# A decoder kernel: the last batch of attention shared out anew, its outputs scaled in parts, the maximum over partitions moved

## The chip, the cores and the metric

The kernel is one program on 1 core of a Trainium2 chip, with its five engines (TensorE, VectorE, ScalarE, GpSimd, and SyncE, which issues the DMAs). The metric is the device time of one execution in microseconds (us): 1484.29 us before, the median of 3 runs (1482.04 to 1485.83). In the profile's rows PE is TensorE, DVE VectorE, ACT ScalarE, POOL GpSimd and SP SyncE.

## The reference

A decoder block on x of 16 batches x 256 rows x 512 columns, with three sublayers, each on the layer norm of x and each added to x:

```python
x = x + attn(_layernorm(x), w_qkv, w_proj)             # 16 heads of 32, causal, weights and activations rounded
x = x + xattn(_layernorm(x), k, fside_S2_0, ctx, ctx, 8)  # a long convolution per head, done as matrix products
x = x + ffn(_layernorm(x), gate_w, up_w, down_w, ...)  # silu(gate) * up, then down, weights in fp8
```

What matters here is how attention ends. The output `out` of a row is divided by the softmax's sum, then `_bitlinear(out, w_proj)` rounds it with a scale of its own per row: `s = 127 / max|out|`, `round(out * s) / s`. So the maximum over all 16 heads of a row must be known before the first element is rounded. The second sublayer starts with the layer norm of the sum, and every product in it needs rows of all 16 batches, the last one too.

## The kernel before

Part 1 is attention. It runs over pairs of heads: batch b has 8 pairs, pair n = 8b + p, 128 in all, the last batch being pairs 120 to 127 (PAIRS = 8, B = 16). Every engine has its own program, written out as a loop over steps t, and a stage of pair n is issued at step t = n + its lag (EXP 9, HIGH 10, LOW 11, WEIGH 12, WEIGHED 13). The order on an engine is that of its loop, and only semaphores tie the engines together. For a pair: TensorE writes transposed scores into a PSUM tile of two banks (`probabilities`, L628 to 652), ScalarE takes the exponential into `pT` (L1433), one engine casts it to fp16, the high part `pH` (ScalarE at L1439 for 7 pairs of 8, VectorE at L1011 for the first), GpSimd subtracts to get the low part `pL` (L1796), TensorE multiplies both with the values (`weigh`, 12 products of 65 columns, L668 and L669), ScalarE copies the result out of PSUM into `oraw` (L1447). `s_kq` is one buffer, so the scores of pair n wait for the exponential of n - 1; `pT` and `pH` are three buffers, `pL` two.

When a batch has its 8 pairs, `finish` on VectorE and ScalarE takes it on: `oraw` has two halves to be added (tile 0 on VectorE, tile 1 on GpSimd, L1801), the product with the reciprocal sums gives `o_sb`, then the maximum, step, reciprocal step, rounding on ScalarE, a transpose on TensorE, a copy on ScalarE, the projection (L684) and on VectorE the addition to x (`add_out`, L1045). The last batch has `finish_last` (VectorE L1048 to 1077, ScalarE L1477 to 1496), which does this for tile 0 (rows 0 to 127) first and then for tile 1, with an `add_out` of the batch before between. ScalarE there computes steps and rounds both tiles before it copies the first transpose.

Then the rows of the last two batches go by DMA into `x_grp`, and part 2 begins: layer norm statistics of head 0 on VectorE (L1182 to 1187), `rstd` and shift on GpSimd (L1845, L1847), scaling on ScalarE (L1608), transpose, and the outer products `kv`: blocks 0 and 1 of head 0 on VectorE (L1194), blocks 2 and 3 on GpSimd (L1866). TensorE multiplies them with the taps (`mix`, L803): of each head first row block 0 (needs kv block 0), then row block 2 (blocks 0, 1, 2 in this order), then 1, then 3, each in two halves.

Beside this, GpSimd takes once the maximum over partitions of 4 numbers (L1837), whose result bounds a scale used much later (`fuse_bound`, seven small VectorE instructions, L1288 to 1301). It comes on GpSimd after the last low part and the last addition, ahead of the layer norm of part 2. Two banks of 128x512 fp32 and a third (`misc`) go round among transposes and projections; who takes one waits for the release of the use three before.

## Time and profile before

| | us |
|---|---|
| median of 3 runs | 1484.29 |
| the profiled execution | 1481.37 |
| its span | 1479.6 |
| TensorE busy | 1391.8 (94%) |
| VectorE busy | 1233.3 (83%) |
| GpSimd busy | 1178.9 (80%) |
| ScalarE busy | 871.6 (59%) |

The span is 1.77 us shorter than its own execution's time. Attention fills the first 462 us or so, the seam to part 2 lies at 462 to 482, and everything later is part 2. Busy shares over the whole span say little about the seam; it is read from the chain of waits and from each engine's rows in order of time, where brackets give the idle time before an instruction and what ended it.

### The profile page before, as it was taken

How to read it: one execution, taken by the hardware profiler on the slowest of the kernel's cores; microseconds unless marked ns; L12 is line 12 of the kernel's file. 1: busy time of each engine (PE TensorE's matmuls, PEld its weight loads, DVE VectorE, ACT ScalarE, POOL GpSimd, SP SyncE). 2: the span in 40 equal slices, each digit the busy share in tenths (PEclk: the TensorE clock that was granted, in tenths of full speed). 3: DMA queues.
4: the chain of work that ended last, by engine and by line, in shares of the span. 5: the costliest groups of instructions: out<-in, count | busy, mean ns of one | idle time of the engine just before them, and what ended most of it. 6: DMA issues, size and time to landing. Idle time of an engine off the chain costs nothing.

```text
span 1479.6 us, 23950 instructions
## 1 busy us (share of the span) xinstructions
PE 1391.8 (94%) x8405; PEld 773.0 (52%) x8405; DVE 1233.3 (83%) x1964; ACT 871.6 (59%) x1437; POOL 1178.9 (80%) x902
## 2 busy tenths in 40 slices
PE   3788999999986997999999999999999999999998
PEld 2677878787863442334444444444444444444443
DVE  6889999999884898899898899899889889888511
ACT  5689999999885123544455545464455446544341
POOL 3389999999985787888888888878887888888532
PEclk9899999999997999999999999999999999999999
DMA  5654646464622533222513421432323232240001
GB/s 193 155 126 117 171 133 172 136 171 122 158 67 75 173 79 88 55 57 64 107 44 72 89 61 43 93 78 50 79 65 77 62 76 57 65 100 15 21 15 29
DMA packets 171587, 133.57 MB, mean 90 GB/s; under 512 B 120500, under 2 KB 124748, under 8 KB 171468
## 3 DMA queue, kind: packets, MB, share of 16 engines
q1 hardware_dynamic: 171276, 131.91, 35.6%
q8 instruction: 67, 1.10, 0.3%
q14 instruction: 52, 0.43, 0.1%
q10 hardware_dynamic: 192, 0.14, 0.1%
HBM read 50.67 MB, written 19.92 MB: 48 GB/s over the span
## 4 chain that ended last, share of the span: by engine, by line
PE 65%; DVE 11%; POOL 8%; issue 7%; ACT 6%; DMA 1%; SPq 0%; POOLq 0%; DVEq 0%; ACTq 0%
PE gu L844 20%; PE gu L858 11%; PE shared_bank L789 9%; POOL pL L1796 3%; PE y L811 3%; PE y L808 3%; PE y L805 3%; PE y L813 3%; PE y L814 3%; DVE blockmax L987 2%; DVE o_sb L1027 2%; PE gu L803 1%; PE y L803 1%; DVE qkt L967 1%; ACT pH L1439 1%
## 5 line engine op out<-in xcount | busy, mean ns | idle before, releaser
L1668 ACT ACTIVATE shared<-shared_bank 128x512 f32<-128x512 f32 x162 | 96.2, 594 | 322.9 <-PE shared_bank L789 322.9
L1219 DVE TENSOR_TENSOR y<-shared,y 128x512 f32<-128x512 f32 x324 | 224.1, 692 | 42.7 <-ACT shared L1668 23.0
L1796 POOL TENSOR_TENSOR pL<-pT,pH 128x768 f16<-128x768 f32 x128 | 216.8, 1696 | 13.6 <-ACT pH L1439 7.7
L1226 DVE TENSOR_REDUCE oT<-z 128x64 f32<-128x512 f32 x256 | 175.6, 686 | 8.7
L844 PE MATMUL gu<-fT,wg 128*128 128x512 f16 x768 | 181.4, 379 | 1.5 <-DMA fT<-fnl 1.5
L844 PE MATMUL gu<-fT,wu 128*128 128x512 f16 x768 | 182.5, 381 | 0.0
L1222 DVE TENSOR_TENSOR z<-y,cT 128x512 f32<-128x512 f32 x236 | 162.4, 688 | 11.0 <-PE y L803 4.4
L1930 POOL TENSOR_TENSOR fuL<-fu,fuH 128x512 f16<-128x512 f32 x96 | 112.0, 1166 | 71.7 <-ACT fuH L1683 71.5
L858 PE MATMUL gu<-wd,fuH 128*128 128x512 f16 x384 | 145.5, 379 | 0.0
L858 PE MATMUL gu<-wd,fuL 128*128 128x512 f16 x384 | 145.5, 379 | 0.0
L1866 POOL TENSOR_TENSOR kv<-vT,cT 128x1024 f32<-128x1024 f32 x70 | 137.8, 1970 | 6.1 <-ACT vT L1623 6.1
L844 PEld LDWEIGHTS gu<-fT,wg 128*128 128x128 f16 x768 | 75.0, 98 | 120.5 <-issue 47.4
L844 PEld LDWEIGHTS gu<-fT,wu 128*128 128x128 f16 x768 | 75.5, 98 | 119.5 <-issue 47.2
L1433 ACT ACTIVATE pT<-s_kq,ws 128x768 f32<-128x768 f32 x128 | 115.0, 898 | 26.9 <-PE s_kq L651 20.2
L987 DVE TENSOR_REDUCE blockmax<-s_qk 128x6 f32<-128x768 f32 x124 | 117.6, 948 | 3.9 <-PE s_qk L621 2.7
L789 PE MATMUL shared_bank<-kv_sum,toep 128*128 128x512 f32 x216 | 111.2, 597 | 0.3 <-POOL kv_sum L1854 0.3
L1854 POOL TENSOR_TENSOR kv_sum<-kv 128x1024 f32<-128x1024 f32 x27 | 63.7, 2360 | 55.2 <-DVE kv L1194 55.2
L637 PE MATMUL s_kq<-pack 128*128 128x128 f16 x768 | 99.4, 220 | 0.0
L1241 DVE SCALAR_TENSOR_TENSOR fu<-gu,cols,sil 128x512 f32<-128x512 f32 x96 | 71.4, 743 | 33.6 <-PE gu L844 33.6
L1789 POOL TENSOR_TENSOR qkhl<-qkt,qkhl 128x512 f16<-128x512 f32 x62 | 83.9, 1354 | 19.2 <-ACT qkhl L1419 19.2
L1439 ACT ACTIVATE pH<-pT 128x768 f16<-128x768 f32 x112 | 94.0, 840 | 0.0
L1194 DVE TENSOR_TENSOR kv<-vT,cT 128x1024 f32<-128x1024 f32 x58 | 75.1, 1297 | 14.2 <-ACT vT L1631 11.5
(231 smaller groups left out, 3561.8 us busy)
## 6 DMA issues: line engine op xcount, KB each, us to landing
pack<-qkhl SPq DMA_DIRECT2D x256, 128.0 KB, 2.6
x_sb<-in_x SPq DMA_DIRECT2D x16, 512.0 KB, 4.0
c_sb<-in_ctx SPq DMA_DIRECT2D x32, 256.0 KB, 4.0
hankel<-in_L_xattn_k SPq DMA_DIRECT2D x32, 256.0 KB, 4.1
out_y<-yo SPq DMA_DIRECT2D x32, 256.0 KB, 2.9
x_grp<-x_scratch SPq DMA_DIRECT2D x30, 256.0 KB, 3.5
x_scratch<-x_sb SPq DMA_DIRECT2D x14, 512.0 KB, 3.0
wraw<-in_L_attn_w_qkv SPq DMA_DIRECT2D x3, 1024.0 KB, 9.6
```

Source lines behind the costliest of these rows:

```text
L789: T.matmul(shared_bank[:], tap(h, (2, 0, 1)[part]), (kv_sum, kv12, kv_sum)[part][:, half * HB:(half + 1) * HB, :, :].rearrange("p b j i -> ...
L844: made = T.matmul(bank[:], (wg, wu)[which][:, cb, ib * P:(ib + 1) * P], fT[:, cb, part, :], start=cb == 0 and part == 0, stop=cb == CB - 1 ...
L858: made = T.matmul(bank[:], src[:, t * P:(t + 1) * P], wd[:, ib, :], start=ib == 0 and part == 0, stop=ib == IB - 1 and part == 1)
L987: V.tensor_reduce(out=blockmax[b % 2][:, p, :], in_=score_tile(n)[:, 0:6, :], op=ALU.max, axis=AXIS.X, negate=True).then_inc(max_done, 1)
L1219: chain.step(V.tensor_tensor(bank[:], shared[2 * part + half][:], bank[:], op))
L1222: V.tensor_tensor(z[:], y, weight, ALU.mult).then_inc(m_zm, 1)
L1226: V.tensor_reduce(out=oT[h % 2][:, lb, own].rearrange("p (b j) -> p b j", b=HB), in_=z[:], op=ALU.add, axis=AXIS.X).then_inc(m_z, 1)
L1433: S.activation(pT[n % NP][:], s_kq[:, 0:6, :], ACT.Exp, scale=ws[:, 4:5]).then_inc(exp_done, 1)
L1439: S.activation(pH[n % NP][:], pT[n % NP][:], ACT.Copy).then_inc(high_act, 1)
L1796: G.tensor_tensor(pL[n % 2][:], pT[n % NP][:], pH[n % NP][:], ALU.subtract).then_inc(low_done, 1)
L1866: G.tensor_tensor(block(h, lb), vT[:, lb, :].rearrange("p (b i) -> p b i", b=B).unsqueeze(2).broadcast_to([P, B, M_POS, M_POS]), cT[h % 2] ...
L1930: G.tensor_tensor(fuL[ib][:], fu[n % 2][:], fuH[:, ib, :], ALU.subtract).then_inc(f_fl, 1)
```

## The change

Pairs 119, 121, 123, 125 and 127 get their low part on VectorE instead of GpSimd, and pair 127 its high part on VectorE instead of ScalarE. From pair 121 on the scores of odd pairs go to `s_qk`, which the row maxima no longer need, so that a pair's scores wait for the exponential two before. VectorE's `finish_last` starts three steps earlier (LAST_AT, after the low part of pair 127) and works on tile 0 in three parts: heads 0 to 7, heads 8 to 13, heads 14 and 15, each with its reciprocal, addition (for the first part on GpSimd, `sum_first`), product and maximum, then a maximum over the three; steps are computed on VectorE too, and outputs lie in `xn`. Its `add_out` of the batch before comes after tile 1. On ScalarE the first transpose is copied ahead of the rounding of tile 1, and the copies of taps and context for head 0 (`turn_taps`, `copy_cT`), once ahead of the last high part, come here; so does `turn_c` on TensorE. GpSimd's maximum over partitions comes behind the layer norm of head 0, and `fuse_bound` at step 8 of part 2.

```diff
-    HIGH_ON_ACT = (1, 2, 3, 4, 5, 6, 7)
+    HIGH_ON_ACT, LAST_HIGH_ON_ACT = (1, 2, 3, 4, 5, 6, 7), (1, 2, 3, 4, 5, 6)
...
+        LAST_AT = B * PAIRS - 1 + LOW
+        LAST_PARTS = ((0, PAIRS // 2), (PAIRS // 2, PAIRS - 1), (PAIRS - 1, PAIRS))
+        LOW_ON_DVE = [n for n in range((B - 1) * PAIRS - 1, B * PAIRS) if n % 2 == 1]
...
+        def scores_tile(n):
+            return s_qk if n > (B - 1) * PAIRS and n % 2 == 1 else s_kq
...
+        FUSE_BOUND_AT, SCALE_DOWN_AT = 8, 20
...
-                w.wait_ge(exp_done, n)
-                T.matmul(s_kq[:, 0:4, :], ident_b[:], mask_kq[:], start=True, stop=False)
+                if n > (B - 1) * PAIRS:
+                    w.wait_ge(exp_done, n - 1)
+                    w.wait_ge(max_done, B * PAIRS)
+                else:
+                    w.wait_ge(exp_done, n)
+                to = scores_tile(n)
...
                     elif k == 0:
+                        turn_c(0, misc1)
                         turn_oq(b, 0)
...
+            def low_part(n):
+                w.wait_ge(*high_done(n))
+                w.wait_ge(pv_pe, n - 1)
+                V.tensor_tensor(pL[n % 2][:], pT[n % NP][:], pH[n % NP][:], ALU.subtract).then_inc(low_last, 1)
...
+                for i, (begin, stop) in enumerate(LAST_PARTS):
+                    first, end = 2 * begin, 2 * stop
+                    w.wait_ge(pv_out, PAIRS * b + stop)
+                    chain.step(V.reciprocal(rl[:, 0, first:end], raw[:, 0, first:end, D]))
+                    if i == 0:
+                        w.wait_ge(o_sum, B)
+                    else:
+                        chain.step(V.tensor_tensor(raw[:, 0, first:end, 0:D], raw[:, 0, first:end, 0:D], raw[:, 0, first:end, VW:VW + D], ALU.add))
+                    chain.wait()
+                    if stop < PAIRS:
+                        chain.step(scale_heads(0, first, end))
+                        chain.wait()
+                        chain.step(V.tensor_reduce(out=inv[:, i:i + 1], in_=xn[:, 0, first * D:end * D], op=ALU.max, axis=AXIS.X,
+                                                   apply_absolute_value=True))
...
+                        chain.step(V.tensor_scalar(am[:, 0:1], am[:, 0:1], inv[:, 0:1], inv[:, 1:2], ALU.max, ALU.max))
+                step_last(0)
...
+                step_last(1)
+                w.wait_ge(c2_done, b)
+                add_out(b - 1, 0)
                 w.wait_ge(c2_done, b + 1)
                 add_out(b, 0)
                 add_out(b - 1, 1)
...
-                if k == 1:
-                    fuse_bound()
...
+                if g == FUSE_BOUND_AT:
+                    fuse_bound()
...
                 for t in range(NT):
-                    w.wait_ge(omax_done, b + t + 1)
-                    S.activation(step[:, t:t + 1], am[:, t:t + 1], ACT.Copy, scale=1.0 / 127.0).then_inc(ostep_done, 1)
                     w.wait_ge(oscale_done, b + t + 1)
...
                     if t == 0:
...
+                        projected(w)
+                        turn_taps(0)
+                    copy_oqT(b, t)
+                    if t == 0:
+                        copy_cT(0, misc1)
...
+            def sum_first():
+                raw, heads = oraw[(B - 1) % 2], slice(0, 2 * LAST_PARTS[0][1])
+                w.wait_ge(pv_out, PAIRS * (B - 1) + LAST_PARTS[0][1])
+                G.tensor_tensor(raw[:, 0, heads, 0:D], raw[:, 0, heads, 0:D], raw[:, 0, heads, VW:VW + D], ALU.add).then_inc(o_sum, 1)
...
-                if t == REDUCE_AT:
-                    w.wait_ge(mx_done, 1)
-                    G.partition_all_reduce(mall[:], mx[:], P, RMAX).then_inc(mall_done, 1)
...
                     G.tensor_tensor(shift, shift, rstd, ALU.mult).then_inc(m_shift, 1)
+                    if h == 0:
+                        w.wait_ge(mx_done, 1)
+                        G.partition_all_reduce(mall[:], mx[:], P, RMAX).then_inc(mall_done, 1)
```


On GpSimd, from the last low parts (pL) to the first kv block of part 2. The rows named ISA are the switches of GpSimd's program and, with mall, the maximum over partitions. Before:

```order
L1796 TENSOR_TENSOR pL<-pT,pH 128x768 x5
L1801 TENSOR_TENSOR oraw<-oraw 128x16x32
L1837 ISA
L1837 ISA mall<-mx 128x4
L1845 ISA
L1845 TENSOR_TENSOR mstat<-mstat,minus_half 128x1
L1847 TENSOR_TENSOR mstat<-mstat 128x1
L1866 TENSOR_TENSOR kv<-vT,cT 128x1024
```

And after the change, same place:

```order
L1839 TENSOR_TENSOR pL<-pT,pH 128x768 x2
L1844 TENSOR_TENSOR oraw<-oraw 128x8x32
L1849 TENSOR_TENSOR oraw<-oraw 128x16x32
L1892 TENSOR_TENSOR mstat<-mstat,minus_half 128x1
L1894 TENSOR_TENSOR mstat<-mstat 128x1
L1897 ISA
L1897 ISA mall<-mx 128x4
L1916 ISA
L1916 TENSOR_TENSOR kv<-vT,cT 128x1024
```

Three low parts are gone from the run of five, and both switches with the maximum now stand between the layer norm (mstat) and the kv block, block 2 of head 0.

On VectorE, from the low part of pair 125 to the rounding step of tile 0, after the change:

```order
L1033 TENSOR_TENSOR pL<-pT,pH 128x768
L1067 SCALAR_TENSOR_TENSOR x_sb<-misc,osmall,x_sb 128x512
L1058 RECIPROCAL osmall<-osmall 128x2
L1028 CAST pH<-pT 128x768
L1067 SCALAR_TENSOR_TENSOR x_sb<-misc,osmall,x_sb 128x512
L1033 TENSOR_TENSOR pL<-pT,pH 128x768
L1078 TENSOR_SCALAR xn<-ones,ws 128x2
L1093 RECIPROCAL osmall<-oraw 128x8
L1081 TENSOR_TENSOR xn<-oraw,osmall 128x256
L1102 TENSOR_REDUCE osmall<-xn 128x1
L1093 RECIPROCAL osmall<-oraw 128x6
L1097 TENSOR_TENSOR oraw<-oraw 128x6x32
```

Before, the two additions to x stood there alone, and after them the undivided work. Now the last low part is queued behind them and ahead of all parts of tile 0, of which the third follows.

On ScalarE, from the last copy of `oraw`, before:

```order
L1447 ACTIVATE oraw<-pv 128x2x130
L1475 ACTIVATE oqT<-misc 128x4x128
L1486 ACTIVATE osmall<-osmall 128x1
L1488 ACTIVATE o_sb<-o_sb,osmall 128x512
L1494 ACTIVATE osmall<-osmall,ws 128x1
L1486 ACTIVATE osmall<-osmall 128x1
L1488 ACTIVATE o_sb<-o_sb,osmall 128x512
L1475 ACTIVATE oqT<-misc 128x4x128
```

And after:

```order
L1495 ACTIVATE oraw<-pv 128x2x130
L1523 ACTIVATE oqT<-misc 128x4x128
L1534 ACTIVATE xn<-xn,osmall 128x512
L1536 ACTIVATE osmall<-osmall,ws 128x1
L1552 ACTIVATE toep<-hankel 128x512
L1523 ACTIVATE oqT<-misc 128x4x128
L1559 ACTIVATE cT<-misc 128x512
L1534 ACTIVATE xn<-xn,osmall 128x512
```

The copy of tile 0's transpose no longer stands behind the step and the rounding of tile 1, but behind the taps' copy.

## Rows read from the trace of the kernel before

**Rows 1.** Busy time by stretch: us from the start, engines, clock, DMA.

```profile
462.00:472.00 10.00, 5.36 (x18) 2.44 (x17) 5.65 (x10) 3.53 (x9) 1.45 (x2) 0.67 0.17 47
482.00:492.00 10.00, 10.00 (x23) 4.37 (x23) 8.17 (x14) 1.41 (x2) 5.38 (x5) 0.74 0.88 282
```

**Rows 2.** Chain of waits, 425 to 500: start us, us, what.

```profile
450.42 4.24 POOL pL L1796 x2
...
475.76 0.71 issue
```

**Rows 3.** GpSimd in order of time: start, us, engine, line, operation, [idle before <-releaser].

```profile
442.21 1.81 POOL L1805 TENSOR_TENSOR fw_raw<-fw_raw,fw_pow 128x768 f32<-128x768 f32 x1
443.98 2.09 POOL L1796 TENSOR_TENSOR pL<-pT,pH 128x768 f16<-128x768 f32 x1
...
450.42 5.83 POOL L1796 TENSOR_TENSOR pL<-pT,pH 128x768 f16<-128x768 f32 x3
...
458.68 1.64 POOL L1796 TENSOR_TENSOR pL<-pT,pH 128x768 f16<-128x768 f32 x1 [0.58 <-ACT pH L1439]
...
469.17 0.39 POOL L1837 PARTITION_ALL_REDUCE mall<-mx  x1 [5.79 <-issue]
476.47 0.59 POOL L1845 TENSOR_TENSOR mstat<-mstat,minus_half 128x1 f32<-128x1 f32 x1 [6.92 <-DVE mstat L1187]
477.14 0.19 POOL L1847 TENSOR_TENSOR mstat<-mstat 128x1 f32<-128x1 f32 x1
480.25 2.99 POOL L1866 TENSOR_TENSOR kv<-vT,cT 128x1024 f32<-128x1024 f32 x1 [2.92 <-ACT vT L1623]
...
486.34 1.95 POOL L1866 TENSOR_TENSOR kv<-vT,cT 128x1024 f32<-128x1024 f32 x1
```

**Rows 4.** GpSimd's switches of its program, one line's query.

```profile
L1837 POOLq MODIFY_POOL_CONFIG  x2: 11/11/11, 463.3 to 463.4; - x2
L1845 POOLq MODIFY_POOL_CONFIG  x2: 82/82/83, 469.5 to 469.5; - x2
```

**Rows 5.** VectorE in order of time, 420 to 500.

```profile
443.77 0.80 DVE L1021 TENSOR_TENSOR oraw<-oraw 128x512 f32<-128x512 f32 x1
450.55 2.60 DVE L1027 TENSOR_TENSOR o_sb<-oraw,osmall 128x1024 f32<-128x1024 f32 x1 [5.98 <-POOL oraw L1801]
...
463.96 0.69 DVE L1063 TENSOR_TENSOR o_sb<-oraw,osmall 128x512 f32<-128x512 f32 x1
...
465.73 0.17 DVE L1070 RECIPROCAL osmall<-osmall 128x1 f32<-128x1 f32 x1 [0.35 <-ACT osmall L1486]
...
475.25 0.18 DVE L1184 BATCH_NORM_AGGREGATE mstat<-mstat 128x2 f32<-128x6 f32 x1
475.47 0.15 DVE L1186 TENSOR_SCALAR mstat<-mstat 128x1 f32<-128x1 f32 x1
...
480.21 4.11 DVE L1194 TENSOR_TENSOR kv<-vT,cT 128x1024 f32<-128x1024 f32 x2 [2.31 <-ACT vT L1623]
```

**Rows 6.** ScalarE in order of time, 420 to 500.

```profile
449.53 0.90 ACT L1433 ACTIVATE pT<-s_kq,ws 128x768 f32<-128x768 f32 x1 [0.97 <-POOL pL L1796]
...
461.85 0.39 ACT L1447 ACTIVATE oraw<-pv 128x260 f32<-128x260 f32 x1
...
465.92 0.72 ACT L1488 ACTIVATE o_sb<-o_sb,osmall 128x512 f32<-128x512 f32 x1 [0.23 <-DVE osmall L1070]
...
468.97 0.58 ACT L1475 ACTIVATE oqT<-misc 128x512 bf16<-128x512 f32 x1
```

**Rows 7.** TensorE in order of time, two stretches.

```profile
469.69 3.57 PE L684 MATMUL misc<-wprojT,oqT 128*128 128x512 bf16 x8 [1.88 <-ACT oqT L1475]
...
481.58 3.75 PE L803 MATMUL y<-kv,toep 128*128 128x512 f32 x4 [2.11 <-DVE kv L1194]
485.12 3.77 PE L803 MATMUL gu<-kv,toep 128*128 128x512 f32 x6
```

**Rows 8.** VectorE in order of time, 500 to 530.

```profile
502.69 0.69 DVE L1222 TENSOR_TENSOR z<-y,cT 128x512 f32<-128x512 f32 x1 [2.02 <-PE y L803]
```

More of the change, by code:

```diff
@@ L675, in turn_oq @@
                 for cb in range(CB):
-                    made = T.transpose(bank[:, cb * P:(cb + 1) * P], o_sb[:, t, cb * P:(cb + 1) * P], ident[:])
+                    made = T.transpose(bank[:, cb * P:(cb + 1) * P], (o_sb if b < B - 1 else xn)[:, t, cb * P:(cb + 1) * P], ident[:])
                 made.then_inc(oqT_pe, 1)
@@ L1073, in finish_last, with scale_heads @@
-                w.wait_ge(ostep_done, b + 2)
-                V.reciprocal(inv[:, 1:2], step[:, 1:2]).then_inc(oscale_done, 1)
+                w.wait_ge(xqT_pe, 2 * B)
+                w.wait_ge(c2_done, b - 1)
+                chain.step(V.tensor_scalar(xn[:, :, C], ones[:, 0:NT], ws[:, 1:2], EPS, ALU.mult, ALU.mult))
+                def scale_heads(t, first, end):
+                    return V.tensor_tensor(xn[:, t, first * D:end * D].rearrange("p (h d) -> p h d", d=D), raw[:, t, first:end, 0:D],
+                                           rl[:, t, first:end].unsqueeze(2).broadcast_to([P, end - first, D]), ALU.mult)
@@ new lines, in step_last @@
+                def step_last(t):
+                    chain.wait()
+                    V.tensor_scalar(step[:, t:t + 1], am[:, t:t + 1], 1.0 / 127.0, None, ALU.mult).then_inc(ostep_done, 1)
+                    w.wait_ge(ostep_done, b + t + 1)
+                    V.reciprocal(inv[:, t:t + 1], step[:, t:t + 1]).then_inc(oscale_done, 1)
+                for i, (begin, stop) in enumerate(LAST_PARTS):
[9 more added lines that the diff above has]
+                        chain.step(scale_heads(0, first, end))
+                        chain.wait()
+                        chain.step(V.tensor_reduce(out=inv[:, i:i + 1], in_=xn[:, 0, first * D:end * D], op=ALU.max, axis=AXIS.X,
+                                                   apply_absolute_value=True))
+                    else:
+                        scale_heads(0, first, end).then_inc(o_mult, 1)
+                        w.wait_ge(o_mult, b + 1)
+                        chain.step(V.tensor_reduce(out=am[:, 0:1], in_=xn[:, 0, first * D:C + 1], op=ALU.max, axis=AXIS.X,
+                                                   apply_absolute_value=True))
+                        chain.wait()
+                        chain.step(V.tensor_scalar(am[:, 0:1], am[:, 0:1], inv[:, 0:1], inv[:, 1:2], ALU.max, ALU.max))
@@ L1141, in vector_program @@
                         low_max(use)
-                if (n := pair(t, HIGH)) is not None and n % PAIRS not in HIGH_ON_ACT:
+                if (n := pair(t, LOW)) in LOW_ON_DVE:
+                    low_part(n)
+                if (n := pair(t, HIGH)) is not None and not high_on_act(n):
                     high_part(n)
@@ L1552, in scalar_program @@
                     copy_weights(i, blocks)
-                if (n := pair(t, HIGH)) is not None and n % PAIRS in HIGH_ON_ACT:
+                if (n := pair(t, HIGH)) is not None and high_on_act(n):
                     high_part(n)
@@ L1820, in gpsimd_program @@
             for t in STEPS:
-                if (n := pair(t, LOW)) is not None:
+                if (n := pair(t, LOW)) is not None and n not in LOW_ON_DVE:
                     low_part(n)
+                if t == LAST_AT:
+                    sum_first()
                 for b, k in batches(t, FINISH, 1):
```

82 lines of the change are left out of this document (31 added, 51 removed).

## The prediction

> **What bounds the kernel now.** I read the chain of waits first, as it says which engine ends each stretch, then each engine's rows in order of time for the seam between attention and part 2, then the granted clock by stretch. In the last pairs the chain runs over GpSimd's low parts [rows 2]: three stand back to back from 450.42 to 456.25 [rows 3], and ScalarE sat idle 0.97 us before an exponential until a low part freed its buffer [rows 6]. The last copy of `oraw` ends at 461.85 + 0.39 = 462.24, the rounding of tile 0 starts at 465.92, its transpose is copied at 468.97 [rows 6], the projections start at 469.69 and TensorE's first product of part 2 at 481.58 [rows 7]. From there TensorE works without a gap (10.00 of 10.00 us busy) [rows 1]. So what lies between 450 and 481 is latency, and a microsecond taken out of it is one off the time, unless something new is late at 481.
>
> **Low parts on VectorE.** GpSimd takes 1.64 us for one [rows 3]. VectorE's row for this form is missing. Its product of 512 columns took 0.69, the addition of 512 took 0.80 [rows 5]; 768 columns are 1.5 times that, 1.03 to 1.20, and I take 1.0, since a fixed part doesn't grow. But the engines don't run freely beside each other. VectorE's addition at 443.77 took 0.80, and the low part that GpSimd began at 443.98 took 2.09 instead of 1.64; the product of 1024 columns at 450.55, beside three low parts, took 2.60, where twice 0.69 is 1.38, and the three took 5.83, where 3 x 1.64 is 4.92 [rows 3, 5]. So I add both engines' operations as one queue. From 442.2 on, until the last low part: two operations on a weight piece, 1.81 each (the one in the rows [rows 3] and its like), three low parts left on GpSimd (122, 124, 126) 4.92, an addition there for which I take 1.1, between VectorE's 0.80 for as many columns and GpSimd's 1.64 for 768, four low parts on VectorE 4.0, its addition 0.80 and product 1.38. That is 15.8, so the last low part ends at 458.0. Products and copy follow in 1.9 us (458.68 + 1.64 = 460.32 to 462.24 before) [rows 3, 6]: 459.9, a gain of 2.3. Ends of the range: if operations also wait for their inputs, 1.1 are left; without any blocking, ScalarE and the chain of pair 127 set the end: the exponential at 449.53 could start 0.97 sooner and the two waits of this size that follow go, 3.4.
>
> By the Trainium skill, SBUF — State Buffer, section "SBUF: two separate sides", VectorE with two SBUF inputs and GpSimd hold one pair of ports in turn, each for a whole instruction. The 2.60 and 2.09 agree with it. By that rule the gain is the 2.3; if the two ran freely, it would be the 3.4.
>
> **The second score buffer and the work off ScalarE.** With `s_kq` alone the scores wait for the exponential before, and ScalarE for them; taps, context copy and one high part stood on ScalarE ahead of pair 127. All this shortens ScalarE's way, which the queue above now outlasts. Its gain is inside the 2.3, and outside it nothing.
>
> **Outputs in parts.** From the end of the last `oraw` copy to the rounding 3.68 us go by (465.92 - 462.24) [rows 6]. After: behind its last low part VectorE has four operations each for parts one and two, some 1.3 us for each part (512 columns take 0.69, the parts have 256 and 192, and tiny operations start 0.22 apart, 475.25 to 475.47 [rows 5]), while TensorE and ScalarE need 1.9 us for pair 127. Then seven tiny dependent operations, 7 x 0.22 = 1.54. Low part to rounding 2.6 + 1.54 = 4.1, less 1.9, is 2.2 against 3.68: gain 1.5; where GpSimd's addition of tile 1 gets in between (1.1), 0.4. VectorE must also finish two additions to x ahead of pair 127's parts: I take 0.7, range 0.2 to 1.5.
>
> **ScalarE's order.** From rounding to projection 469.69 - 465.92 = 3.77 us [rows 6, 7], in which the copy of the transpose stood behind tile 1's step and rounding. Without them: rounding 0.72, transposes 0.9 (512 columns take 3.57 / 8 = 0.45, fp32 has two passes [rows 7]), copy 0.58, hand-overs 0.4 = 2.6. But the projection's bank is now the one that `add_out` of batch 14 frees, and that stands behind tile 1 on VectorE: 0.2 + 0.69 + 0.69 + 0.4 + 0.7 + 0.2 = 2.9. Gain 0.8, range 0.5 to 1.1. `turn_c` stands ahead of the transpose on TensorE and runs while the rounding is awaited; taps and context copy fit beside transposes and projection, and if the latter were late, it would be 0.6. SyncE's issues of the last rows keep their order and wait for the same additions; nothing is queued differently there.
>
> **The maximum over partitions.** Before, GpSimd was through at 463.4, the first switch is at 463.3, and the maximum starts at 469.17 after 5.79 us of idle time that has no releaser; the second switch is at 469.5, and the next GpSimd instruction starts at 476.47 [rows 3, 4]. That one waited for VectorE, ready by 475.76: the chain has 0.71 us of "issue" there which nothing else explains [rows 2]. I read it as the end of a second load like the first, from 469.56 to at most 476.47: 5.79 and 6.9 us. Its cover was the wait for the last batch. Moving the maximum behind the layer norm gives back 0.6 (0 to 0.7). But now both loads are queued ahead of kv block 2 of head 0. Call M the end of the shift (477.14 + 0.19 = 477.33 [rows 3]). Block 2 began at M + 2.92 and took 2.99 beside VectorE; alone it takes 1.95 [rows 3]. Now 5.79 + 0.39 + 6.9 = M + 13.1, done at M + 15.05. TensorE's row block 0 starts at 481.58 = M + 4.25. A product has two passes here: four for the two halves of block 0, and six for a half of row block 2, from 485.12 = M + 7.8, of which the fifth needs kv block 2 [rows 7]. It stands there at M + 10.3 (two thirds of 3.77) and waits until M + 15.2: a stall of 4.9 us where there was none. VectorE's own kv blocks end sooner without GpSimd beside them, which helps nobody. All of TensorE's following work moves by it. GpSimd's backlog (block 3, 1.95, and the skip's product) is worked off before head 1's blocks can start, as these wait for a transpose behind the stalled products.
>
> The clock adds to it. The first products ran at the lower of the two levels, 1.2 of 2.4 GHz: granted 0.67 in 462 to 472, 0.74 in 482 to 492 [rows 1], after TensorE had been half idle. Four passes took 3.75, 0.94 each, and at the upper level it would be 0.47 [rows 7]. A stall of 4.9 us invites a second such stretch. Cost of the move: 4.9, plus 0 to 3, and I take 5.8; the least is 0, if the second load is short, and the most 7.8.
>
> The Trainium skill, GPSIMD Engine Reference, section "Instruction dispatch", has a load of about 6 us (5.95) which the first call after a switch pays. The 5.79 agrees; the 476.47 doesn't, if the load began only with that call, as it would be near 481.7. By two loads of 5.95 the stall would be 4.1 instead of 4.9.
>
> `fuse_bound` moves to step 8: seven tiny operations, 7 x 0.22 = 1.5 us, into a place where VectorE idled 2.02 us [rows 8]. Nothing; without that cover 1.5.
>
> **Sum.** Gains 2.3 + 0.7 + 0.8 + 0.6 = 4.4 (1.8 to 6.7); cost 5.8. Net +1.4: the profiled execution's 1481.37 would be 1482.8, and on the median of the runs, 2.9 higher, 1484.29 + 1.4 = 1485.7.
>
> **Rivals.** (A) The second load is short or absent. Then block 2 begins at M + 6.3 and is done at M + 8.3, ahead of its use at M + 10.3: no stall, -4.4, 1479.9 (1477.6 to 1482.5). For it: only 0.71 us of an edge speak of that load. Against it: the first is as plain as can be, and a switch stands ahead of both. (B) Slower: the clock after the stall. TensorE stands until M + 15.2 and then runs at the lower level as long as it did from 481.58, some 6 us for 3 us of work: cost 7.8. It decides wherever the gains stay under 3.3, and with 2.3 the time is +5.5, 1489.8. For it: 0.67 and 0.74 after lesser gaps; against it: it needs weak gains too. (C) The change doesn't do what it says: odd low parts only change the engine in one queue, VectorE's additions to x get late by as much, and attention's pairs and parts together end 1.0 sooner, not 3.0. With the stall 5.8 - 1.0 - 0.8 - 0.6 = +3.4, 1487.7; without it -2.4, 1481.9.
>
> **How the numbers follow.** What this kernel's measurement can tell from no change is 0.3%, 4.5 us, so 1479.8 to 1488.7. The forecast (stall, net -2 to +4.5) has 0.47, of it 0.45 same and 0.02 slower. A 0.27: being on the edge, 0.16 faster, 0.11 same. B 0.12, slower. C 0.14: 0.10 same, 0.02 on either side. That is faster 0.18, same 0.66, slower 0.16; I move 0.04 from same to faster, since the gains reach to 6.7. The range 1478.5 to 1490 leaves out a tenth at each end; the forecast's own is 1482.3 to 1488.7.
>
> **What would show it.** In the changed kernel, from the same start: the last `oraw` copy ends near 459.9 and tile 0's rounding starts near 462.9; a gap on TensorE inside the first six passes of row block 2, of 4 to 5 us, ended by GpSimd's kv; that kv starts 13 us behind the shift. The forecast is wrong if it starts within 7 us of the shift (A), if passes behind the stall still take over 0.8 us (B), or if pair 127's copy ends after 461 (C).

## The result, and the profile after

The changed kernel takes 1489.20 us in the median of 6 runs (1487.30 to 1491.39), the kernel before 1485.06 (6 runs on the same chip): ratio 1.0029, 95% interval 1.0018 to 1.0041, so some 4.3 us slower. The forecast was 1485.7, in a range of 1478.5 to 1490. The profiled executions took 1489.15 (span 1487.4) and 1481.37.

The two profiles are out of step by 1.50 us ahead of everything that the prediction speaks of: the last copy of `nmT` starts at 441.06 before and at 442.56 after, and so does the exponential ahead of it. They are apart from early in attention on (the third such copy starts at 86.91 and 88.25), long before the first changed instruction. Times of after are therefore compared less 1.50, or counted from this copy. ScalarE in order of time, before (first fence) and after:

```profile
441.06 0.36 ACT L1426 ACTIVATE nmT<-misc 32x256 bf16<-32x256 f32 x1
```

```profile
442.56 0.36 ACT L1474 ACTIVATE nmT<-misc 32x256 bf16<-32x256 f32 x1
...
462.03 0.39 ACT L1495 ACTIVATE oraw<-pv 128x260 f32<-128x260 f32 x1
...
464.98 0.72 ACT L1534 ACTIVATE xn<-xn,osmall 128x512 f32<-128x512 f32 x1 [1.44 <-DVE osmall L1088]
...
466.44 0.60 ACT L1523 ACTIVATE oqT<-misc 128x512 bf16<-128x512 f32 x1
```

The last copy of `oraw` starts 19.47 behind the `nmT` copy, where it was 20.79 [rows 6]: 1.3 us sooner. The rounding of tile 0 is 2.4 sooner (22.42 for 24.86), the copy of its transpose 4.0 sooner (23.88 for 27.91). GpSimd in order of time:

```profile
473.55 0.20 POOL L1894 TENSOR_TENSOR mstat<-mstat 128x1 f32<-128x1 f32 x1
480.73 0.39 POOL L1897 PARTITION_ALL_REDUCE mall<-mx  x1 [6.99 <-issue]
488.79 1.94 POOL L1916 TENSOR_TENSOR kv<-vT,cT 128x1024 f32<-128x1024 f32 x1 [7.67 <-issue]
```

The shift ends at M = 473.75, which is 5.1 us sooner than the 477.33 of [rows 3] when the 1.50 is taken off. But then comes what [rows 3, 4] had spread over the wait for the last batch: 6.99 us of idle time without a releaser, the maximum, 7.67 us of the same, and only then kv block 2, done at 490.73 = M + 16.98. The program switches stand at the beginning of both gaps (two rows of the query by line):

```profile
L1897 POOLq MODIFY_POOL_CONFIG  x2: 11/11/11, 473.7 to 473.7; - x2
```

```profile
L1916 POOLq MODIFY_POOL_CONFIG  x2: 83/83/83, 481.1 to 481.1; - x2
```

TensorE in order of time, the rows that answer to [rows 7]:

```profile
467.57 1.90 PE L702 MATMUL misc<-wprojT,oqT 128*128 128x512 bf16 x8 [1.16 <-DVE x_sb L1067]
...
477.53 3.75 PE L820 MATMUL y<-kv,toep 128*128 128x512 f32 x4 [2.11 <-DVE kv L1242]
481.08 2.68 PE L820 MATMUL gu<-kv,toep 128*128 128x512 f32 x4
490.78 2.07 PE L820 MATMUL gu<-kv,toep 128*128 128x512 f32 x2 [7.03 <-POOL kv L1916]
...
493.50 4.14 PE L820 MATMUL gu<-kv,toep 128*128 128x512 f32 x6
...
501.36 7.03 PE L820 MATMUL y<-kv,toep 128*128 128x512 f32 x16
```

TensorE did four of the six passes of row block 2's first half, stood 7.03 us for GpSimd's kv, and did the rest slowly: two passes 2.07, the next six 4.14, where the six of the second half took 2.74 before. From the sixteen passes at 501.36 on (495.62 before) TensorE's rows are alike for the next 34 us. I use M and the start of these sixteen passes as two marks: from M to them 18.29 us before (495.62 - 477.33), 27.61 after. That is 9.3 lost behind M and 5.1 won ahead of it: +4.2, beside a measured +4.3.

That the two agree so well is partly luck. The profiled executions themselves are 7.8 us apart: 1.5 ahead, 4.2 in the seam, and 2.1 behind it, where the rest of the span from the sixteen passes on is 986.0 us after and 984.0 before. This rest lies between 984.0 and 986.1 in the profiles of all the kernels here. The lowest two are the kernel before and run 9, which is the same kernel behind the seam, so whether a part of the 2.1 belongs to the change stays open.

By stretch (us, then busy time of TensorE, its weight loads, VectorE, ScalarE and GpSimd, granted clock, DMA share, GB/s):

```profile
482.00:492.00 10.00, 2.97 (x6) 1.16 (x5) 0.70 (x2) 0.40 (x1) 3.13 (x4) 0.67 0.44 148
492.00:502.00 10.00, 10.00 (x26) 4.88 (x25) 6.08 (x9) 2.56 (x4) 6.11 (x4) 0.78 0.35 93
```

TensorE was busy 2.97 of 10 us in the first. In steps of 2 us the granted clock (the third number from the end) can be told apart:

```profile
484.00:486.00 2.00, 0.00 (x0) 0.00 (x0) 0.00 (x0) 0.00 (x0) 0.00 (x0) 1.00 1.03 332
...
494.00:496.00 2.00, 2.00 (x3) 0.67 (x2) 1.81 (x3) 0.35 (x1) 1.10 (x1) 0.50 0.44 95
```

The upper level (1.00) was still granted when TensorE had gone idle at 483.7; it fell near 486 to the lower of the two levels (0.50: 1.2 of 2.4 GHz), stayed there until TensorE had worked again from 490.78 to about 496, and was 1.00 again from 498 on. Before, 492 to 502 had 1.00 throughout.

### The profile page after: what moved, and what is told of

It reads as the page before. It is cut to its first block, busy times and chain, and to the rows that moved or that the text cites. A ratio compares the mean times of both kernels' runs of the same rounds, so it can differ in the third digit from the quotient of the medians.

```text
span 1487.4 us, 23962 instructions
## 1 busy us (share of the span) xinstructions
PE 1390.7 (94%) x8405; PEld 772.8 (52%) x8405; DVE 1243.8 (84%) x1982; ACT 870.1 (59%) x1434; POOL 1172.4 (79%) x898
## 4 chain that ended last, share of the span: by engine, by line
PE 62%; DVE 13%; POOL 8%; issue 8%; ACT 7%; DMA 2%; SPq 1%; POOLq 0%; DVEq 0%; ACTq 0%
PE gu L861 20%; PE gu L875 11%; PE shared_bank L806 9%; PE y L828 3%; PE y L825 3%; PE y L822 3%; PE y L830 3%; PE y L831 3%; POOL pL L1839 2%; DVE blockmax L1004 2%; DVE o_sb L1049 2%; DVE z L1270 1%; DVE qkt L984 1%; PE misc L702 1%; DVE osmall L1055 1%
## 5 line engine op out<-in xcount | busy, mean ns | idle before, releaser
L1839 POOL TENSOR_TENSOR pL<-pT,pH 128x768 f16<-128x768 f32 x123 | 206.7, 1682 | 15.7 <-ACT pH L1487 8.4
L1481 ACT ACTIVATE pT<-s_kq,ws 128x768 f32<-128x768 f32 x124 | 111.3, 898 | 24.0 <-PE s_kq L669 19.3
L650 PE MATMUL s_kq<-pack 128*128 128x128 f16 x744 | 95.8, 219 | 0.0
```

The source lines that it names most:

```text
L1481: S.activation(pT[n % NP][:], scores_tile(n)[:, 0:6, :], ACT.Exp, scale=ws[:, 4:5]).then_inc(exp_done, 1)
L1839: G.tensor_tensor(pL[n % 2][:], pT[n % NP][:], pH[n % NP][:], ALU.subtract).then_inc(low_done, 1)
```

## The experiments

All kernels do the whole computation of the reference. Ratios are to the kernel before, which ran beside them on the same chip.

**1. The maximum back at its old place, all else changed.**

```diff
+                if t == REDUCE_AT:
+                    w.wait_ge(mx_done, 1)
+                    G.partition_all_reduce(mall[:], mx[:], P, RMAX).then_inc(mall_done, 1)
...
-                    if h == 0:
-                        w.wait_ge(mx_done, 1)
-                        G.partition_all_reduce(mall[:], mx[:], P, RMAX).then_inc(mall_done, 1)
```

> The changed kernel, with the maximum over partitions put back to its old place (behind the last sum of parts); all else of the change stays. Theory 1 (two program loads in a row stand ahead of kv block 2 of head 0 and stall TensorE; everything else of the change gains): the stall of 7.0 us ahead of row block 2 goes, the shift waits for the end of the second load at about 476.7 instead and ends 0.6 to 1.3 us earlier than in the kernel before, and the time is 1484, about 1 below the kernel before and 5 below the changed one. Rival 1 (the stall has another reason, such as fuse_bound at step 8 or VectorE's kv blocks): the stall stays and the time is near the changed kernel's, +4 on the kernel before. Rival 2 (the maximum at its old place needs no second load on the way): about -5.

Measured: 1482.37, ratio 0.9979 (0.9969 to 0.9990), 3.1 us faster than before and 7 faster than the change as a whole. GpSimd in its profile:

```profile
470.38 0.39 POOL L1887 PARTITION_ALL_REDUCE mall<-mx  x1 [6.20 <-issue]
477.78 0.59 POOL L1895 TENSOR_TENSOR mstat<-mstat,minus_half 128x1 f32<-128x1 f32 x1 [7.01 <-issue]
478.45 0.19 POOL L1897 TENSOR_TENSOR mstat<-mstat 128x1 f32<-128x1 f32 x1
```

The stall is gone, and rival 1 with it. The gaps of 6.20 and 7.01 us are at the old place too, and the `rstd` now waits for the second one alone (its releaser is "issue", not VectorE as in [rows 3]). The shift ends 35.47 behind the `nmT` copy (36.27 before), the 0.8 that theory 1 expects; from M to the sixteen passes it is 17.53, another 0.8 less, which I had not expected. Rival 2 is out by the second gap. The size was missed: theory 1 said 1 us below the kernel before, and the interval is 1.5 to 4.6 us. The traces up to the sixteen passes show 1.6 of the 3.1.

**2. No program load at all: the maximum on TensorE and VectorE.**

```diff
+                if t == MAX_AT:
+                    bank = misc1.take("max", w, (mall_done, 1))
+                    w.wait_ge(mx_done, 1)
+                    T.transpose(bank[0:4, 0:P], mx[:], ident[:]).then_inc(mx_done, 1)
+                if t == MAX_AT + 2:
+                    w.wait_ge(mx_done, 3)
+                    T.matmul(misc1.of["max"][:, 256:260], ones[0:4, :], mcol[0:4, 4:8], start=True, stop=True).then_inc(mx_done, 1)
...
+                if t == MAX_AT + 1:
+                    w.wait_ge(mx_done, 2)
+                    chain.step(V.tensor_reduce(out=mcol[0:4, 0:1], in_=misc1.of["max"][0:4, 0:P], op=ALU.max, axis=AXIS.X))
+                    chain.wait()
+                    V.tensor_scalar(mcol[0:4, 4:8], ident[0:4, 0:4], mcol[0:4, 0:1], None, ALU.mult).then_inc(mx_done, 1)
+                if t == MAX_AT + 3:
+                    w.wait_ge(mx_done, 4)
+                    V.tensor_copy(mall[:], misc1.of["max"][:, 256:260]).then_inc(mall_done, 1)
...
-                        G.partition_all_reduce(mall[:], mx[:], P, RMAX).then_inc(mall_done, 1)
```

> The changed kernel, with the maximum over partitions computed without GpSimd's custom instruction: a transpose of mx by TensorE, a maximum over the free axis on VectorE, the result spread over a 4x4 diagonal and multiplied by ones on TensorE, copied on VectorE, some 20 steps ahead of attention's end. No GpSimd program is loaded any more. Theory 1: shift ends 5.1 us earlier than in the kernel before (as in the changed one), no stall behind it: -5 on the kernel before, 1480, range 1478 to 1481.5. Rival (kv block 2 is late for another reason than the loads): the stall stays, time within 1 us of the changed kernel's.

Measured: 1480.00, ratio 0.9961 (0.9946 to 0.9977), 5.3 us by the medians, 5.8 by the ratio. GpSimd:

```profile
473.93 0.19 POOL L1910 TENSOR_TENSOR mstat<-mstat 128x1 f32<-128x1 f32 x1
476.58 2.99 POOL L1929 TENSOR_TENSOR kv<-vT,cT 128x1024 f32<-128x1024 f32 x1 [2.46 <-ACT vT L1682]
```

M is 31.24 behind the `nmT` copy, as in the changed kernel (31.19), and kv block 2 begins 2.5 behind M. So the rest of the change is worth 5 us, and the loads alone turned it over.

**3. Only the maximum moved (and `fuse_bound`), nothing else.**

```diff
-                if k == 1:
-                    fuse_bound()
...
+                if g == 8:
+                    fuse_bound()
...
-                if t == REDUCE_AT:
-                    w.wait_ge(mx_done, 1)
-                    G.partition_all_reduce(mall[:], mx[:], P, RMAX).then_inc(mall_done, 1)
...
+                    if h == 0:
+                        w.wait_ge(mx_done, 1)
+                        G.partition_all_reduce(mall[:], mx[:], P, RMAX).then_inc(mall_done, 1)
```

> The kernel before, with only two moves of the change: the maximum over partitions behind the first layer norm of part 2 on GpSimd, and fuse_bound at step 8 on VectorE. Theory 1: the full cost of the two loads, stall 7.0 plus 2.3 for the clock behind it, less 0.6 for the edge of the second load: +8.7 us on the kernel before, 1493.8. Rival (the stall costs only what I forecast, and the clock nothing): +4.9 to +5.8, 1490 to 1491. Rival (the gains of the attention part cost the rest, not the loads): within 1 us of the kernel before.

Measured: 1493.47, ratio 1.0058 (1.0039 to 1.0076): +8.2 us by the medians, +8.6 by the ratio. GpSimd:

```profile
478.85 0.19 POOL L1844 TENSOR_TENSOR mstat<-mstat 128x1 f32<-128x1 f32 x1
486.14 0.39 POOL L1847 PARTITION_ALL_REDUCE mall<-mx  x1 [7.10 <-issue]
494.12 1.94 POOL L1866 TENSOR_TENSOR kv<-vT,cT 128x1024 f32<-128x1024 f32 x1 [7.60 <-issue]
```

From M (479.04) to the sixteen passes (505.44) it takes 26.40, 8.1 more than before. The move costs by itself about what theory 1 said. The rival of no effect is out; the rival of 4.9 to 5.8 us only touches the lower end of the interval (5.8), and the 8.1 of the trace speaks against it. M lies 36.83 behind the `nmT` copy here, 0.6 later than before instead of 0.6 sooner: the last `oraw` copy is 21.99 behind it and not 20.79, with the same instructions up to there. So one trace of a kernel can differ from another by 1.2 us in attention's last pairs.

**4. As 2, all low parts on GpSimd.** The edit is `LOW_ON_DVE = []`.

> As the run without GpSimd's maximum, and in addition all low parts stay on GpSimd (none on VectorE); second score buffer, outputs in parts and ScalarE's order stay. Theory 1 (VectorE and GpSimd work as one queue, moving the low parts between them gains 1.3 us as the changed kernel's trace shows it): 1.3 slower than that run, -3.8 on the kernel before. Rival (my forecast's size, 2.3): 2.3 slower than that run. Rival (nothing but the engine changes in one queue): the same as that run within 0.5.

Measured: 1481.46, ratio 0.9979 (0.9967 to 0.9991): 1.5 us above run 2 by the medians, 2.7 by the ratios, whose intervals overlap. ScalarE:

```profile
464.89 0.39 ACT L1511 ACTIVATE oraw<-pv 128x260 f32<-128x260 f32 x1 [1.37 <-PE pv L688]
...
468.94 0.72 ACT L1550 ACTIVATE xn<-xn,osmall 128x512 f32<-128x512 f32 x1 [2.54 <-DVE osmall L1096]
```

The last copy of `oraw` is 20.42 behind the `nmT` copy at 444.47 (19.55 in run 2) and the rounding 24.47 (22.49). The low parts on VectorE are worth 0.9 at the copy but 2.0 at the rounding, since in run 4 GpSimd's addition for the first part (`sum_first`) stands behind the last low part and VectorE waits 0.49 us for it. The 0.9 is within what two traces of the same instructions differ by (run 3, and run 10 below), the 2.0 is not, so I take "nothing" as ruled out by the rounding; between 1.3 and 2.3 the times can't tell.

**5. As 2, one score buffer.**

```diff
-            return s_qk if n > (B - 1) * PAIRS and n % 2 == 1 else s_kq
+            return s_kq
...
-                if n > (B - 1) * PAIRS:
-                    w.wait_ge(exp_done, n - 1)
-                    w.wait_ge(max_done, B * PAIRS)
-                else:
-                    w.wait_ge(exp_done, n)
+                w.wait_ge(exp_done, n)
```

> As the run with the maximum on TensorE and VectorE, with one score buffer to the end (every pair's scores go to s_kq and wait for the exponential before). Theory (GpSimd's and VectorE's queue sets the pace of the last pairs, ScalarE's way is outlasted): no more than 0.5 slower than that run, -5 on the kernel before. Rival (the second buffer carries part of the gain, since scores, exponential and high part follow each other for each pair): 1 to 2 slower than that run, -3.5 to -4.

Measured: 1479.14, ratio 0.9956 (0.9942 to 0.9970), against 0.9961 with two. No gain of the second buffer shows. Whether it does slight harm is not shown either: without it the last copy of `oraw` is 18.42 behind the `nmT` copy, 1.1 sooner, and the rounding 22.08, 0.4 sooner, but run 10's trace has 18.12 and 22.18 with two buffers.

**6. The kernel before, with the maximum on TensorE and VectorE (the edit of 2).**

> The kernel before, with nothing changed but the maximum over partitions, which TensorE and VectorE compute some 20 steps ahead of attention's end, so that GpSimd loads no program. Theory 1 (before the change the end of the second load held up the first shift by 0.6 to 0.7 us only): -0.6 on the kernel before, 1484.7. Rival (the loads, or DMA that they share with others, cost elsewhere too): -2 or more.

Measured: 1483.23, ratio 0.9986 (0.9976 to 0.9996), 2.1 us; the near end of the interval lies at the expected 0.6, and the rival's "2 or more" fits the middle. In the trace M is 35.80 behind the `nmT` copy, 0.5 sooner, as expected; from M to the sixteen passes it is 17.31 instead of 18.29, and there the six passes of row block 2 took 2.79 instead of 3.77 [rows 7], with everything ahead of them alike. So how long the lower clock level lasts differs by about 1 us between these traces, and the profile of before was at the long end. The same stretch is 16.9 to 18.2 in the other traces without a stall, so this 1 us needs no loads, and it may be the second 0.8 of run 1 too. It does not explain the medians: the two profiled executions are 1481.37 (before) and 1482.67 (run 6), the other way round. A place where the loads cost more than the 0.5 does not show in the traces (the rest of the span from the sixteen passes on is 984.0 before and 985.6 in run 6), but the rival is not refuted by the times.

**7. Late weight loads.**

```diff
-                if g < 2 * CB:
-                    gate_up_load(g)
+                if 8 <= g < 8 + 2 * CB:
+                    gate_up_load(g - 8)
```

> The changed kernel, with the eight loads of gate and up weights (384 KB each, four of which were issued between 475.9 and 479.7, in the middle of GpSimd's first program load) issued from step 8 on, behind the stall. Theory 2 (DMA traffic lengthens the program loads from 5.8 and 6.9 to 7.0 and 7.7): the loads shrink by 1 to 2 us together, the stall from 7.0 to 5 to 6, and the time lies 1 to 2 below the changed kernel's. Rival (the length of the loads does not hang on DMA traffic): idle time ahead of the maximum and of kv stays within 0.3 of 6.99 and 7.67, time within 0.5 of the changed kernel's.

Measured: 1489.30, ratio 1.0024 (1.0011 to 1.0036), as the changed kernel. GpSimd, and the two gaps as windows:

```profile
483.10 0.39 POOL L1897 PARTITION_ALL_REDUCE mall<-mx  x1 [7.55 <-issue]
490.68 1.94 POOL L1916 TENSOR_TENSOR kv<-vT,cT 128x1024 f32<-128x1024 f32 x1 [7.19 <-issue]
```

```profile
475.40:483.10 7.70, 4.39 (x9) 2.15 (x10) 4.74 (x8) 2.04 (x3) 0.15 (x1) 0.63 0.89 235
483.10:490.70 7.60, 2.32 (x4) 0.64 (x3) 1.38 (x2) 0.00 (x0) 0.41 (x2) 0.72 0.07 15
```

The same windows for the changed kernel, and the first gap of the kernel before:

```profile
473.70:480.70 7.00, 3.80 (x8) 1.93 (x9) 4.41 (x8) 2.04 (x3) 0.04 (x1) 0.65 0.81 209
481.10:488.80 7.70, 2.65 (x5) 0.84 (x3) 1.38 (x2) 0.00 (x0) 0.03 (x2) 0.72 0.70 239
```

```profile
463.40:469.20 5.80, 1.65 (x7) 0.76 (x5) 4.18 (x8) 2.17 (x6) 0.03 (x1) 0.79 0.12 37
```

The second gap had a DMA share of 0.07 (0.70 in the changed kernel) and still took 7.19 (7.67). The sum of both did not shrink, as theory 2 wanted: 6.99 + 7.67 = 14.66 after, 7.10 + 7.60 = 14.70 in run 3, 7.55 + 7.19 = 14.74 here. So a second gap without traffic did not make the pair shorter. But the edit did not empty the first gap: its share rose from 0.81 to 0.89, and it took 7.55 instead of 6.99, more than the 0.3 that the rival allows. At the old place the first gap had shares of 0.12 (before) and 0.29 (run 1), and the sums there are 12.7 (at most) and 13.2. Traffic in the first gap goes along with the longer sums, then, and no run here has tested whether it causes them.

**8. TensorE kept busy in the gaps ahead of part 2 (on run 2).**

```diff
                         project_out(b, 1)
+                        w.wait_ge(pv_out, B * PAIRS)
+                        for i in range(10):
+                            T.matmul(pv[:, 0:P], ident[:], ident[:], start=True, stop=True)
...
             part1_done(w)
+            for i in range(8):
+                T.matmul(row_bank(0)[:, 0:P], ident[:], ident[:], start=True, stop=True)
```

> As the run with the maximum on TensorE and VectorE, with products that nobody reads in two gaps of TensorE: ten of 128 columns behind the last projection (472.1 to 475.2) and eight ahead of part 2's first product (475.8 to 477.9). Theory 3 (the first products of part 2 run at the lower clock because TensorE was half idle ahead of them): the first four passes take 1.9 instead of 3.75 us, and the time is up to 2.4 below that run, -7.5 on the kernel before. Rival (the clock is not won back by these few products): four passes take 3.75 still, the extra products delay TensorE's transposes by 0 to 0.6, and the time is 0 to 0.6 above that run.

Measured: 1476.82, ratio 0.9938 (0.9923 to 0.9953), 8.3 us below the kernel before and the fastest by its ratio. TensorE:

```profile
474.05 2.39 PE L757 MATMUL pv<-ident 128*128 128x128 f32 x20
477.29 0.63 PE L793 MATMUL misc<-ident,v_sb 128*128 128x128 f32 x4 [0.85 <-ACT v_sb L1672]
...
480.46 1.88 PE L831 MATMUL y<-kv,toep 128*128 128x512 f32 x4
482.18 2.74 PE L831 MATMUL gu<-kv,toep 128*128 128x512 f32 x6
```

Theory 3 holds: the first four passes take 1.88 us, the next six 2.74. From M (476.24) to the sixteen passes (491.64) it is 15.40, where run 2 has 17.45: 2.05 in the traces, 3.2 by the medians of the two runs.

**9. The same gaps filled in the kernel before.** The edit is that of 8.

> The kernel before, with products that nobody reads in two gaps of TensorE ahead of part 2 (ten and eight of 128 columns). Theory 3 (the clock of part 2's first products hangs on the gaps ahead, whatever the rest of the kernel): the first four passes take 1.9 instead of 3.75, the first six 2.7 instead of 3.8, and the time is 2 to 3 below the kernel before, 1482.5. Rival (it needs the changed kernel's shorter tail): 0 to 0.6 slower.

Measured: 1480.40, ratio 0.9975 (0.9964 to 0.9985): 4.8 us by the medians, 3.7 by the ratio. The passes take 1.88 and 2.84, and from M to the sixteen passes it is 15.29, 3.0 less than before. It needs nothing of the change.

**10. The stall filled.**

```diff
                     for kb in range(lb + 1):
+                        if h == 0 and s == 2 and kb == lb:
+                            for i in range(24):
+                                T.matmul(shared_bank[:, 0:P], ident[:], ident[:], start=True, stop=True)
```

> The changed kernel, with 24 products of 128 columns that nobody reads put into TensorE's stall, between the fourth and the fifth pass of row block 2 (about 6 us of 7.0). Theory 1 with the clock (of the 9.3 that the loads cost, 7.0 are the stall and 2.3 the lower clock behind it): passes behind the stall take 0.45 instead of 0.69 to 1.04, and the time is 1.5 to 2.3 below the changed kernel's, +2.2 on the kernel before. Rival (the clock falls whatever stands in the stall): as the changed kernel within 0.5, or above it where the products run over the stall's end.

Measured: 1487.71, ratio 1.0023 (1.0012 to 1.0033); its interval overlaps that of the changed kernel. GpSimd, then TensorE:

```profile
482.43 0.39 POOL L1900 PARTITION_ALL_REDUCE mall<-mx  x1 [5.66 <-issue]
491.68 1.94 POOL L1919 TENSOR_TENSOR kv<-vT,cT 128x1024 f32<-128x1024 f32 x1 [8.86 <-issue]
```

```profile
486.35 5.52 PE L822 MATMUL shared_bank<-ident 128*128 128x128 f32 x48
493.67 1.12 PE L823 MATMUL gu<-kv,toep 128*128 128x512 f32 x2 [1.80 <-POOL kv L1919]
...
495.07 2.74 PE L823 MATMUL gu<-kv,toep 128*128 128x512 f32 x6
```

The two passes take 1.12 instead of 2.07, the six 2.74 instead of 4.14, and from M to the sixteen passes it is 24.75 instead of 27.61. The trace gives 2.9 us back, the times 1.5 by the medians and 0.9 by the ratios: the direction is shown by the passes, the size is not settled. The gaps split as 5.66 + 8.86 here, sum 14.52.

**11. As 2, tile 0 in one part.**

```diff
-        LAST_PARTS = ((0, PAIRS // 2), (PAIRS // 2, PAIRS - 1), (PAIRS - 1, PAIRS))
+        LAST_PARTS = ((0, PAIRS),)
```

`sum_first` goes with it; VectorE adds all heads of tile 0.

> As the run with the maximum on TensorE and VectorE, with tile 0 of the last outputs handled in one part as before the change (VectorE adds, scales and takes the maximum of all 16 heads behind pair 127's copy). Forecast's term: 0.7 slower than that run. The traces' term (2.56 us from the last copy to the rounding instead of 3.68): 1.1 slower, and since VectorE's low parts then end earlier, perhaps nothing of it: range 0 to 1.1. Rival (parts are what brings most of the gain): 2 or more.

Measured: 1480.62, ratio 0.9969 (0.9958 to 0.9981): 0.6 by the medians and 1.2 by the ratios above run 2, with overlapping intervals. In the trace the rounding is 23.58 behind the `nmT` copy instead of 22.49: 1.1.

**12. All together: run 8 with one score buffer, and five products instead of eight in the second gap.**

> The changed kernel with three further edits together: the maximum on TensorE and VectorE, one score buffer, and products that nobody reads in two gaps of TensorE, of which now ten stand in the first and five in the second (eight held up the first real product by 0.4). Theory: the second score buffer adds nothing (its copy of pair 127 came 1.1 later by the traces), filling the gaps gives 2 to 2.5, so -8.5 on the kernel before, 1476.6, and 0.4 to 1 below the run that filled the gaps with two score buffers. Rival (the trace's 1.1 of the score buffer is spent on VectorE, which rounds tile 0 only 0.4 earlier): as that run within 0.5.

Measured: 1476.57 in the median of 9 runs (1475.29 to 1482.37), ratio 0.9956 (0.9941 to 0.9971). The median is run 8's (1476.82) within 0.3, the ratio is 0.0018 above its ratio; two of the nine lie near 1482, one of them the profiled one, and its TensorE shows a part of why:

```profile
475.40 1.86 PE L699 MATMUL misc<-wprojT,oqT 128*128 128x512 bf16 x4 [0.78 <-ACT oqT L1540]
477.05 3.31 PE L753 MATMUL pv<-ident 128*128 128x128 f32 x20
480.20 0.60 PE L789 MATMUL misc<-ident,v_sb 128*128 128x128 f32 x4
```

The lower level had lasted through the projections here (four passes 1.86, not 1.02), the ten products took 3.31 instead of 2.39, and they held up the transpose of `v_sb`: it starts 3.00 behind M (477.20), where it is 1.05 behind in run 8. From M to the sixteen passes it is 17.21 instead of 15.40, 1.8 of the 5.8 us by which this execution is above the median; the rest is not explained. Filling pays when the products are done before the real work is ready, and at the lower level they aren't. Whether one score buffer adds to run 8 stays open.

## Why the prediction was off where it was

The change was forecast at +1.4 and came to +4.3; the time is 3.5 us above the forecast of 1485.7. The mechanism that it names is the right one (rival A, no second load, is ruled out by the 7.67 us gap and by run 3), but both large terms were short, the cost by 3.5 and the gains by 0.7, and the difference is what is missing. The cost of 9.3 lies above its own upper bound of 7.8, and the time lies above the forecast's own range (1482.3 to 1488.7). That it still falls inside 1478.5 to 1490 owes something to luck: the range was held open upwards for rival B, and the gains made up for 0.7 of the cost.

**Gains: 4.4 forecast, 5.1 in the traces, 5.3 in run 2.** By part:
- Low parts: 2.3 forecast, 1.3 found at the last `oraw` copy. The step that failed is "I add both engines' operations as one queue": I counted the operations that share ports, and left out what VectorE does alone. From 451.69 to 460.43 it has no gap:

```profile
451.69 2.70 DVE L1049 TENSOR_TENSOR o_sb<-oraw,osmall 128x1024 f32<-128x1024 f32 x1 [1.02 <-POOL oraw L1849]
454.42 1.22 DVE L1055 TENSOR_REDUCE osmall<-o_sb 128x2 f32<-128x1026 f32 x1
455.56 2.15 DVE L1033 TENSOR_TENSOR pL<-pT,pH 128x768 f16<-128x768 f32 x1
457.63 0.74 DVE L1067 SCALAR_TENSOR_TENSOR x_sb<-misc,osmall,x_sb 128x512 f32<-128x512 f32 x1
...
458.37 0.53 DVE L1028 CAST pH<-pT 128x768 f16<-128x768 f32 x1
458.82 0.74 DVE L1067 SCALAR_TENSOR_TENSOR x_sb<-misc,osmall,x_sb 128x512 f32<-128x512 f32 x1
459.49 0.94 DVE L1033 TENSOR_TENSOR pL<-pT,pH 128x768 f16<-128x768 f32 x1
```

The maximum (1.22), two additions to x (0.74 each) and pair 127's high part (0.53) are 3.2 us that my 15.8 didn't hold. VectorE's own queue set the end, with the waits for GpSimd inside it: one low part took 2.15, the other 0.94. The last low part ended at 460.43, less 1.50 at 458.9, not at 458.0. The upper bound of this term, 3.4, was also misread: of the exponential's waits that follow the 0.97, one is 0.97 and the next 0.42, so the three are 2.4.
- Outputs in parts: 0.7 forecast, 1.1 in the traces (from the last `oraw` copy to the rounding 2.56 instead of 3.68), and 1.1 in run 11. VectorE was late from the low part, but so was pair 127, so the parts still ran in its shadow. The line between this term and the one above is not firm. In run 10's trace, with the same instructions up to there, the last copy is 18.12 behind the `nmT` copy at 444.97 (2.7 sooner than before) and the rounding 22.18, so that from the one to the other nothing is won:

```profile
463.09 0.39 ACT L1498 ACTIVATE oraw<-pv 128x260 f32<-128x260 f32 x1 [0.64 <-PE pv L687]
...
467.15 0.72 ACT L1537 ACTIVATE xn<-xn,osmall 128x512 f32<-128x512 f32 x1 [2.99 <-DVE osmall L1091]
```

  Together the two terms are 2.4 and 2.7 in the two traces, against 3.0 forecast.
- ScalarE's order: 0.8 forecast, 1.2 found: 467.57 - 464.98 = 2.59 to the projection instead of 3.77. It waited for the bank of `add_out` as forecast (1.16 us idle, ended by `x_sb`). The eight passes of the projection then took 1.90, not 3.57 as in [rows 7], at the upper clock level; the last addition of tile 0 waits for the first four of them, so that is 0.8 more, which no term had.
- The edge of the second load: 0.6 forecast, 0.5 in the trace of run 6.

**Cost: 5.8 forecast, 9.3 in the traces.**
- The loads: 5.79 + 0.39 + 6.9 = 13.1 was read from before; it was 6.99 + 0.39 + 7.67 = 15.05. The first gap was copied from its old place, the second was only bounded by 6.92. They were undersized by 1.2 and 0.8. In the three kernels with the switches behind the shift that keep TensorE's stall empty the gaps add up to 14.7; at the old place to 13.2 (run 1) and at most 12.7 (before). What makes them 1.5 to 2 longer behind the shift is open: run 7 speaks against DMA traffic in the second gap, and the first was not tested.
- The stall: 4.9 forecast, 7.03 found, by these 2.0.
- The clock: 0.9 taken out of 0 to 3, 2.3 found (9.3 - 7.0). By rows: the passes and transposes behind the stall took 2.8 longer than before, and the transposes of `v_sb` ahead of part 2 took 0.63 instead of 1.09, as they ran at the upper level. Rival B had the right mechanism and came nearest with 1489.8, but that is luck: it has a stall of 4.9 with 2.9 of clock instead of 7.0 with 2.3, and gains of 2.3 instead of 5.1. Its sign, passes over 0.8 us behind the stall, came (2.07 for two); its condition, gains under 3.3, did not. A longer stall took that condition's place, and no case of mine had one.
- `fuse_bound` at step 8: nothing, as forecast, but not by the cover that was named. It did not fall into the 2.02 us of [rows 8] but behind them, and its seven instructions took 2.3 us (the last one 1.19, where it took 0.23 before). The product `z` behind them starts 12.50 after the sixteen passes instead of 10.26, and TensorE's rows don't move for it.

**Rival C** (low parts only change engines): its sign, pair 127's copy after 461, did come by the clock of the trace (462.42), but less 1.50 it is 460.9, just below. It had pairs and parts together at 1.0 us; they are 2.4 in the trace, and run 4 shows 2.0 for the low parts at the rounding. It falls.

The Trainium skill, GPSIMD Engine Reference, section "Instruction dispatch", has about 6 us paid by the first call after a switch. What the runs show differs in two ways: the switch back to the ordinary program has a gap as long (7.0 to 8.9), and in [rows 3] and run 1 the gap runs from the switch on, while the instruction behind it still waits for others. The measurement decides: 13 to 15 us for the pair, counted from the first switch.

## What to carry to other kernels

The maximum over partitions switches GpSimd's program there and back, and each switch began a gap of 5.7 to 8.9 us in which GpSimd did nothing. Before such an instruction is moved, look for what stands behind it on GpSimd and who waits for that; here it was nearly free only where GpSimd waited for the last batch anyway, and five small instructions on TensorE and VectorE do without it.

Where TensorE was half idle ahead of its busiest stretch, the first passes there cost double (3.75 us for four instead of 1.88). A few products that nobody reads won back 2 to 3 us in the traces, as long as they end before the real work is ready; a gap's length at the lower level decides how many fit.

When work is moved to an engine, write down its whole queue over the stretch, its reductions and casts too, and not only what it shares with the other engine.

## What the hardware showed that was not expected

- Behind the shift the two gaps around the maximum split differently from run to run (6.99 + 7.67, 7.10 + 7.60, 7.55 + 7.19, 5.66 + 8.86), with a sum of 14.5 to 14.7. The row of the maximum is not a sure sign of where one load ends.
- A short VectorE instruction can pay for a whole GpSimd one. The addition of 64 columns took 0.89 us beside GpSimd's addition of 1.07, and 0.21 without it (run 5):

```profile
462.76 0.89 DVE L1097 TENSOR_TENSOR oraw<-oraw 128x64 f32<-128x64 f32 x1
```

```profile
462.54 0.21 DVE L1101 TENSOR_TENSOR oraw<-oraw 128x64 f32<-128x64 f32 x1
```
- Executions with the same rows up to the seam differ in how long the lower clock level lasts: 16.9 to 18.3 us from M to the sixteen passes in seven kernels that are alike there (before, runs 1, 2, 4, 5, 6 and 11). It may be a part of what single runs of one kernel differ by (1481.09 to 1488.38 in 32 runs of the kernel before); that was not tried.
